# PoolE adds the halves of y_act, one transpose turns all coefficients, ScalarE takes the second norm's variance, and the order of a step is new

## The reference

```python
# 1: linear causal attention over a norm of the channels (eps 1e-6)
q, kv = Wq @ ln_c(x) + bq, Wkv @ ln_c(x) + bkv      # 128 -> 128 and 128 -> 256
Q, K  = elu(q) + 1, elu(k) + 1                       # 8 heads of 16
den = 1.0 / (sum_d(Q * cumsum(K, tokens)) + 1e-10)
num_t = Q_t @ (sum over s <= t of K_s V_s^T)         # causal
x = x + num * den
# 2: mixture of 8 experts, the best 2 of a softmax, over a norm of each token (eps 1e-5)
t = tokens(x); xf = (t - mean(t)) / sqrt(var(t) + eps)
probs = softmax(xf @ gate_w + router_gamma); combine = top 2 of probs, the rest 0
eo = xf @ expert_w[e] + expert_b[e]
t = t + sum_e combine[e] * (gam[e] * eo + bet[e])    # gam, bet are means over instructions
```

## Time and profile before

| what | value |
|---|---|
| times of the runs | 754.3, 754.41, 756.66 us; median 754.41 |
| profiled execution | 755.91 us |
| its span, first to last instruction | 754.1 us |
| PE busy | 717.1 us, 95% |
| DVE busy | 685.9 us, 91% |
| ACT busy | 409.9 us, 54% |
| POOL busy | 397.8 us, 53% |
| DMA | 30.29 MB, 14.4% of 16 engines |
| chain that ended last | PE 91%, DVE 4%, POOL 2% |
| mean granted TensorE clock | 0.982 |

### The profile page before, as it was taken

One profiled execution on the slowest core, in us unless ns is written; L12 is line 12 of the kernel. 1 busy time (PEld: TensorE's weight loads), 2 busy tenths in 40 slices (PEclk: granted clock), 3 DMA queues, 4 the chain that ended last, 5 costly groups with the idle time before them and its releaser, 6 DMA issues.

```text
span 754.1 us, 23195 instructions
## 1 busy us (share of the span) xinstructions
PE 717.1 (95%) x8137; PEld 624.0 (83%) x8137; DVE 685.9 (91%) x2550; ACT 409.9 (54%) x1261; POOL 397.8 (53%) x639
## 2 busy tenths in 40 slices
PE   4767999999999999999999999999999999999986
PEld 2666888888888888888888888888888888888875
DVE  4567999999999999999999999999999999999984
ACT  1122666655555666666665555555555555555544
POOL 5145555555555555555555555555555555555520
PEclk9769999999999999999999999999999999999999
DMA  5101111111111111111111111111111111111101
GB/s 129 33 15 30 42 40 35 37 40 37 39 37 42 42 42 42 42 42 42 42 42 42 42 42 42 42 42 42 42 42 42 42 42 42 42 30 29 30 16 29
DMA packets 60214, 30.29 MB, mean 40 GB/s; under 512 B 2160, under 2 KB 60176, under 8 KB 60176
## 3 DMA queue, kind: packets, MB, share of 16 engines
q1 hardware_dynamic: 60176, 29.79, 14.4%
HBM read 20.34 MB, written 9.44 MB: 39 GB/s over the span
## 4 chain that ended last, share of the span: by engine, by line
PE 91%; DVE 4%; POOL 2%; ACT 1%; issue 1%; DMA 1%; SPq 0%; DVEq 0%; ACTq 0%; POOLq 0%
PE bank L877 11%; PE bank L915 10%; PE bank L894 9%; PE bank L916 9%; PE bank L917 9%; PE bank L933 8%; PE bank L901 4%; PE bank L909 4%; PE bank L884 4%; PE bank L853 3%; PE bank L854 3%; PE bank L855 3%; PE bank L860 3%; PE bank L847 2%; PE bank L866 2%; PE bank L935 2%
## 5 line engine op out<-in xcount | busy, mean ns | idle before, releaser
L574 DVE TENSOR_TENSOR probs<-bank,tri 128x512 f32<-128x512 f32 x288 | 184.9, 684 | 10.2 <-PE bank L877 4.7
L397 ACT ACTIVATE y_act<-bank,scale 128x128 f32<-128x128 f32 x576 | 159.4, 383 | 2.5
L915 PE MATMUL bank<-e_high,x_high 128*128 128x512 f32 x288 | 124.0, 431 | 1.1 <-DVE o L803 1.1
L916 PE MATMUL bank<-e_low,x_high 128*128 128x512 f32 x288 | 113.7, 395 | 0.0
L917 PE MATMUL bank<-e_high,x_low 128*128 128x512 f32 x288 | 113.5, 394 | 0.0
L311 POOL TENSOR_TENSOR qn<-feat,rden 128x512 f32<-128x512 f32 x36 | 38.2, 1061 | 116.4 <-DVE rden L672 116.4
L416 ACT ACTIVATE x_high<-x 128x512 fp32r<-128x512 f32 x36 | 22.8, 633 | 137.0 <-DVE x L664 137.0
L592 DVE SCALAR_TENSOR_TENSOR y_dve<-bank,scale,y_dve 128x128 f32<-128x128 f32 x288 | 92.4, 343 | 0.0
L580 DVE SCALAR_TENSOR_TENSOR qkv<-bank,rstd,b_qkv 128x384 f32<-128x384 f32 x144 | 86.8, 605 | 5.1 <-POOL rstd L301 2.6
L387 ACT ACTIVATE k_odd<-bank,parity 128x512 f32<-128x512 f32 x36 | 24.7, 687 | 114.4 <-PE bank L860 114.4
L933 PE MATMUL bank<-ident,y_act 128*128 128x128 f32 x576 | 80.8, 273 | 1.6 <-ACT y_act L397 1.6
(11 more groups left out here) (139 smaller groups left out, 1764.5 us busy)
## 6 DMA issues: line engine op xcount, KB each, us to landing
x<-in_x SPq DMA_DIRECT2D x36, 256.0 KB, 3.3
x_res<-in_x SPq DMA_DIRECT2D x36, 256.0 KB, 3.2
out<-o SPq DMA_DIRECT2D x36, 256.0 KB, 2.4
beta_raw<-in_L_ffn_beta_w SPq DMA_DIRECT2D x1, 512.0 KB
e_raw<-in_L_ffn_expert_w SPq DMA_DIRECT2D x1, 512.0 KB
w_raw<-in_L_conv_Wkv SPq DMA_DIRECT2D x2, 64.0 KB, 2.4
b_qkv<-in_L_conv_bkv SPq DMA_DIRECT2D x1, 128.0 KB, 4.4
w_raw<-in_L_conv_Wq SPq DMA_DIRECT2D x1, 64.0 KB, 2.6
```

Of the source, the lines that this page charges most:

```text
L397: last = nc.scalar.activation(y_act[:, p, u, e], bank[EXPERTS_AT[u][0]][:, 128 * e:128 * e + 128], ACT.Copy, scale=scale[:, p, u, e:e + 1])
L574: return tt(probs[:, half, i].rearrange("p u e t -> p (u e) t"), bank[SCORES_AT[half][i]][:].rearrange("p (n t) -> p n t", t=T), tri[:].un ...
L915: mm(out, x1_high[:, p, u], e_high[:, w], start=True, stop=False)
L916: mm(out, x1_high[:, p, u], e_low[:, w], start=False, stop=False)
```

## The change

- **Halves.** After `weigh_four` PoolE adds `y_act[2:4]` to `y_act[0:2]` (`add_halves`, 128 x 256 values, one for each unit), and `turn_y` transposes two of `y_act` and one of `y_dve`.
- **Coefficients.** `coef3` is packed (4 units x 4 x 8 columns = 128), so `turn_coef` is one transpose, and `coef_t` 128 x 128. `bias` becomes four fp32r matmuls of 128 columns, each with weights `bias_rows[:, u]` that are zero outside its unit's rows. They are prepared at the start.
- **Variance.** `id_gate` holds the centring matrix for the identity, so the transposed x1 is already without its mean. ScalarE squares each unit with `accum_out` into `mv2` (`variance`); VectorE's `parts` and `moments` of the second norm go.
- **Order.** `LAGS` is 9: x is loaded at lag 0, `turn_x` is at lag 2, `project` 3, `features` 4, keys and denominators 5, scores and values 6, x1 and the router 7, experts and output 8. The banks and the order of every engine are new.

```diff
+REST_COLS = 2 + 6 + EXPERTS + 1 + 1 + 2 * 4
+REST_PSUM = REST_COLS + 1
-LAGS = 6
+LAGS = 9
-AT = dict(x=4, kv=3, att=6, x1_a=6, x1_b=4, k=1, q=7, coef=0, out=1)
-PROJ_AT = (4, 0, 3, 2)
-SCORES_AT = ((3, 7, 2, 0), (0, 5, 6, 7))
-EXPERTS_AT = ((4, 2), (6, 5), (1, 1), (2, 3))
+AT = dict(x=1, kv=5, att=0, x1_a=0, x1_b=5, k=7, q=4, coef=7, out=3)
+PROJ_AT = (2, 6, 2, 1)
+SCORES_AT = ((7, 3, 1, 6), (2, 6, 5, 3))
+EXPERTS_AT = ((4, 1), (4, 3), (0, 7), (5, 4))
+SUMS = 2
@@ PoolE
+            def add_halves(p, u):
+                return tt(y_act[:, p, u, 0:2], y_act[:, p, u, 0:2], y_act[:, p, u, 2:4], ALU.add)
+                    need(pool, "y_act_1", n + 1)
+                    add_halves(p, 1).then_inc(S["y_sum_1"], 1)
...
@@ ScalarE
+            def variance(p, units):
+                for u in units:
+                    last = nc.scalar.activation(squares[:, u], x1_units[u], ACT.Square, scale=CH ** -0.5,
+                                                accum_out=mv2[:, p, u, 1:2])
+                return last
+                if g[7]:
+                    n, p = g[7].i, g[7].par
+                    need(act, "x1_turned", n + 1)
+                    variance(p, (IN_N,)).then_inc(S["x1_var_b"], 1)
+                    need(act, "x1_var_b", n + 1)
+                    nc.scalar.activation(lg_raw[:, IN_N], bank[AT["x1_b"]][:, T:WIDE], ACT.Copy)\
+                        .then_inc(S["lg_raw_b"], 1)
+                    variance(p, range(IN_N)).then_inc(S["x1_var_a"], 1)
...
@@ VectorE, weights
-                make(copy(id_gate[:, 0:T], ident[:]))
+                make(copy(id_gate[:, 0:T], centre[:]))
+                dve.wait_ge(S["rest_pe"], 4)
+                turned = bank[WEIGHTS_AT[3]][:, 0:EXPERTS]
+                make(copy(bias_high[:], turned))
+                for u in range(U):
+                    make(copy(bias_cols[:, u, u, 0:2], bias_high[:].bitcast(F32).unsqueeze(1).broadcast_to([128, 2, EXPERTS])))
+                    make(tt(bias_cols[:, u, u, 2], turned, bias_high[:].bitcast(F32), ALU.subtract))
+                dve.wait_ge(S["rest_pe"], 5)
+                make(copy(bias_rows[:].rearrange("p u d -> p (u d)"), bank[WEIGHTS_AT[0]][:]))
...
@@ PE
             def turn_coef(p):
+                return transpose(bank[AT["coef"]][:, 0:T], coef3[:, p].rearrange("p u s e -> p (u s e)").bitcast(F32), ident[:])
+            def bias(p):
                 for u in range(U):
-                    last = transpose(bank[AT["coef"]][0:3 * QUAD, T * u:T * u + T], coef3[:, p, u].bitcast(F32), ident[:])
-            def bias(p):
-                return mm(bank[AT["out"]][:], e_bias3[:], coef_t[:, p], start=True, stop=False, skip_group_check=True)
+                    last = mm(bank[AT["out"]][:, T * u:T * u + T], bias_rows[:, u], coef_t[:, p], start=(u == 0),
+                              stop=False, skip_group_check=True)
             def turn_y(p, u):
-                for e in range(4):
+                for e in range(SUMS):
```

More of the change, by code:

```diff
@@ L177, in program @@
         names = ("consts setup first_loaded rest_loaded first_pe first_dve rest_pe rest_dve x_eps x1_eps "
[4 rows of a table removed]
-                 "rank_b qkv_0 rank_b_max soft_scaled den_eps hot_b x1 hot_ab rden scale coef qkv_3 x_moments "
[5 rows of a table removed]
-                 "k_sum_3 x_rstd k_sum_4 k_sum_5 k_sum_6 k_sum_7 qk qn state coef_low x_low x1_rstd ").split()
[3 rows of a table added]
+                 "kv_new rank_b_max x1 qkv_2 probs_01 hot_b probs_03 soft_scaled hot_ab x_moments scale "
[3 rows of a table added]
+                 "second feat_0 rank_b soft x_parts out k_sum_0 x1_high q_t exps_0 x1_var_b lg_raw_b x1_var_a "
[3 rows of a table added]
+                 "x_low ").split()
         S = {n: sem(n) for n in names}
@@ new lines, in step @@
+                if g[2]:
+                    p = g[2].par
+                    act.wait_ge(x_loaded[p], 16 * (g[2].half + 1))
+                    nc.scalar.activation(x_high[:, p], x[:, p], ACT.Copy).then_inc(S["x_high"], 1)
+                if g[8]:
+                    n, p = g[8].i, g[8].par
+                    need(act, "coef_turned", n + 1)
+                    need(act, "bias", n - 1)
+                    nc.scalar.activation(coef_t[:, p], bank[AT["coef"]][:, 0:T], ACT.Copy).then_inc(S["coef_t"], 1)
@@ new lines, in step @@
+                if g[7]:
+                    n, p = g[7].i, g[7].par
+                    need(dve, "values_1", n + 1)
+                    need(dve, "values_0", n + 1)
+                    dve.wait_ge(x_res_loaded[p], 16 * (g[7].half + 1))
+                    need(dve, "out", n - 1)
+                    tt(flat(x1, p), bank[AT["att"]][:], flat(x_res, p), ALU.add).then_inc(S["x1"], 1)
+                if g[4]:
+                    n, p = g[4].i, g[4].par
+                    need(dve, "proj_2", n + 1)
+                    add_bias(p, 2).then_inc(S["qkv_2"], 1)
@@ L879, in scores @@
                 return last
-            def from_state(p):
-                for u in range(U):
-                    last = mm(bank[AT["att"]][:, T * u:T * u + T], state[:, U * p + u], q_t[:, p, u],
-                              start=(u == 0), stop=False, skip_group_check=True)
-                return last
             def values(p, half):
@@ L895, in values, with from_state @@
                                       probs[:, half, i, v, e], start=False, stop=(e == 1), skip_group_check=True)
+                return last
+            def from_state(p):
+                for u in range(U):
+                    last = mm(bank[AT["att"]][:, T * u:T * u + T], state[:, U * p + u], q_t[:, p, u],
+                              start=(u == 0), stop=False, skip_group_check=True)
                 return last
@@ new lines, in step @@
+                if g[7]:
+                    n, p = g[7].i, g[7].par
+                    need(pe, "kv_new", n + 2)
+                    need(pe, "x1", n + 1)
+                    if k is not None:
+                        need(pe, "y_act_3", n - 1)
+                    turn_x1(p).then_inc(S["x1_turned"], 1)
+                if g[8]:
+                    n, p = g[8].i, g[8].par
+                    need(pe, "q_t", n + 3)
+                    need(pe, "x1_low", n + 1)
+                    if k is not None:
+                        need(pe, "y_one_3", n)
+                        need(pe, "y_dve_32", n)
+                    experts(p, 1, 0).then_inc(S["experts_10"], 1)
@@ L954, in step @@
                 if g[3]:
                     n, p = g[3].i, g[3].par
+                    need(pe, "x_low", n + 1)
+                    need(pe, "probs_10", n - 2)
+                    if k is not None:
+                        need(pe, "qkv_2", n)
+                    project(p, 0).then_inc(S["proj_0"], 1)
+                if g[8]:
+                    n, p = g[8].i, g[8].par
+                    need(pe, "y_act_0", n + 1)
+                    if k is not None:
+                        need(pe, "q_t", n + 3)
+                    experts(p, 3, 1).then_inc(S["experts_31"], 1)
@@ L1003, in step @@
+                    key_values(p).then_inc(S["kv"], 1)
+                if g[3]:
+                    n, p = g[3].i, g[3].par
+                    need(pe, "probs_11", n - 2)
                     if k is not None:
```

850 lines of the change are left out of this document (410 added, 440 removed), and 18 rows, old and new, of the table names.

## The result

The changed kernel takes 774.61 us (median), the kernel before 755.28 in the same session: a ratio of 1.026 (95% interval 1.021 to 1.030), slower where I had forecast 721.5. The profiled execution of the changed kernel has a span of 774.6 us.

A forecast was written before the change was run, and what follows sets the result against it. PE's own instruction stream was taken as the bound, VectorE close behind. First `o` 95.4 + 29 steps x 18.5 + drain 85.7 + end 3.5 = 721.1 us span, so 721.5 us; range 705 to 744.

The forecast's parts named there:

- PE's stream: PE's instructions in one step: 19.21 - 0.87 (y transposes) - 0.33 (coefficients) + 0.3 (bias) + 0.1 (new order) = 18.4 us.
- The holds: VectorE instructions with two SBUF inputs held by PoolE: 0.5 to 1 us a step in all, said to cost nothing.
- the three instructions that I saw brush against additions: rank_a, second and soft on VectorE, expected to meet PoolE's additions, for 0.5 to 1 us in all.
- VectorE's idle time before `o`: VectorE idles about 1 us before the x parts and before `o`; up to there, being held was to cost nothing.
- My slow rival: VectorE held by PoolE becomes the bound: two full hits a step give 19.5 us (754 us), four 787 us; chance 0.08.
- Does it wait?: Check whether the other engines make PE wait: 0.1 us a step allowed, bounds 0 and 0.6; likeliest step 18.5 us.
- the two narrow starts, x1 and lg_raw_b: VectorE's x1 and causals, ScalarE's square b and lg_raw_b, both ending about when scores 1 starts; 0.1 us a step allowed.
- ScalarE: Four squares with an accumulator on ScalarE, 0.2 to 0.5 us each; its busy share goes from 60% to 65 to 70%.
- Fill: Time to the first `o`: 95.4 us against 89.7, bounds 90 and 102, with PE's first project at about 29.
- Drain: The last six, emptier steps: 17.9, 15.8, 15.5, 14.5, 11.5 and 10.5 us, 85.7 in all, estimates within 6 us.
- Square's table: Rival: Square needs another ScalarE table, two loads a step, PE waits 1.5 to 2.6 us, 780 us or more; chance 0.03.
- PoolE's price: Each of PoolE's four additions of 256 elements takes 0.73 us, 2.9 us more in a step.

The follow-up runs named there:

- experiment 1: The changed kernel with VectorE's lg2 moved ahead of features 1: 747.61 us, ratio 0.989 against the kernel before.
- experiment 3: The kernel before, old order, with the edits one by one: halves 776.89 us, variance (the squares) 777.42, coefficients 754.39, all three 789.53.
- experiments 1 and 4: Experiment 1, and as the other the changed kernel with PoolE's addition into state moved behind k_sum 1: 753.48 us, ratio 0.996.
- experiment 6: The changed kernel with PE's project 3 and key_values ahead of project 0: 765.95 us; with VectorE's y_dve_02 also earlier: 745.10 us.
- the extra matmuls: Experiment 1's kernel with matmuls that nobody reads added where PE idled up to step 7: 742.92 us, ratio 0.982.

## Why the prediction was wrong, point by point

- **PE's stream (0.2 us off, and two errors that cancel in part).** A unit's three transposes now start 0.32 us apart from the next unit's (421.06 and 421.38 below), for 0.54 in the earlier trace rows. The four bias matmuls take 400.97 - 400.58 = 0.39 us; I took 0.53 (0.23 and +0.3) from bounds of 0.44 and 0.90, so even the lower bound was high. PE needs 18.67 us a step once the hold is gone (experiment 1), of which it is idle for 0.17 (99.1 of 100 us busy), for my 18.4. With 0.39 for the bias my sum would have been 19.21 - 0.87 - 0.33 + 0.06 = 18.07. By this estimate the new order costs some 0.4 us, where I had 0.1 and an upper bound of 0.3; which edges cost it isn't traced.

```profile
400.58 0.56 PE L972 MATMUL bank<-coef_t,bias_rows 128*128 128x128 f32 x4
400.97 0.30 PE L893 MATMUL bank<-ident,x 128*128 128x128 f32 x1
```
```profile
421.06 0.38 PE L981 MATMUL bank<-ident,y_act 128*128 128x128 f32 x2
421.27 0.27 PE L983 MATMUL bank<-ident,y_dve 128*128 128x128 f32 x1
421.38 0.38 PE L981 MATMUL bank<-ident,y_act 128*128 128x128 f32 x2
```

- **The holds (the step that failed).** I had the row that shows one and the price, 1.0 us each. I counted only the three instructions that I saw brush against additions, and not each of the fifteen against each PoolE instruction of the step; lg2 against `state` isn't among them. I then covered the sum with VectorE's idle time before `o`. That idle time lies behind the place where PE waits: `qkv_0` stands right after lg2, and project 2 needs it. The small holds by additions that I priced are there, 0.16 us each at lgm and rank_a, and cost nothing: experiment 1 has them too. The one that I left out was 1.1 us in one place and made the step 0.9 us longer (experiments 1 and 4). My slow rival (two full hits a step, chance 0.08) asked for two full hits where one was enough, since it took VectorE's work for the only thing that matters and not its order.
- **Does it wait? (an omission.)** I followed the two narrow starts, x1 and lg_raw_b, and they hold: PE waits 0.2 us before scores 1. add_bias 3's wait for `key_values` I didn't follow. It costs nothing by itself (experiment 1) but brings lg2 beside `state` (experiment 6).
- **ScalarE (right in the new order).** A square takes 0.279 us and its accumulator another 0.208, in my range of 0.2 to 0.5 each. In the old place the same squares cost 0.67 us a step (experiment 3), and in the new order PE has no wait for them in 100 to 700 us.
- **Fill (mechanism right, size off by 14 us).** The first project came at 31.85 for 29, which is within what traces with the same preparation differ by (27.5 to 31.9); steps 3 to 5 took 24.6 for 20, step 6 17.2 for 14.7, step 7 17.4 for 14.3, step 8 18.4 for 17.4. I had summed chains at middle durations, while PE ran at half clock in part and waited, 2.64 us in each of steps 6 and 7, until causal 10 was through. In written-out steps the hand-made order is paid for though the work that it makes room for isn't there. Without the hold the first `o` came 2.2 us earlier, with the extra matmuls 3.7 more, and with key_values earlier too 5.3; the remaining 6 to 7 us against my 95.4 stay unexplained.
- **Drain (off by 8.6 us).** The last six steps took 94.3 us for 85.7; no run was made for this.
- **Square's table, PoolE's price.** Both as forecast: one load, 0.734 us for 0.73.

With the hold taken away the kernel is 1% faster than before and not the 4% forecast: 30 steps give 16 us (19.21 - 18.67 each) and the emptier last five 9 (74.9 for 84.2), but the first `o` comes 17.5 us later (107.2 for 89.7).

## What to carry to other kernels

When an edit puts work on PoolE, or moves anything there, list each VectorE instruction that can be held against each PoolE instruction of the step, and for each overlap ask what stands behind it on VectorE and who waits for that; idle time later in the step is no cover. An order by hand that shows no such meeting is a part of the kernel's speed: the three edits in the old order made it 4.5% slower, by holds and by squares that stand ahead of a copy, and two neighbours swapped in the new one were worth 27 us. A deeper pipeline's fill has waits and a clock of its own; durations of the middle are too short for it.

## What was not expected of the hardware

- The hold ends with PoolE's instruction, whatever the size of VectorE's: 0.18 us became 1.27 (beside a 1.49 us instruction) and 0.34 (beside 0.74). It takes tensor_scalar with one SBUF input too, and neither reductions nor reciprocals.
- It goes both ways: `state` took 1.28 us by itself and 1.34 or 1.49 us in turn when `features` was running as it began (1.57 or 1.72 in most steps of experiment 1).
- Reading the accumulator is an instruction of its own on ScalarE, 0.208 us; square and reading come every 0.25 us (417.87, 418.03, 418.12 in experiment 3's kernel).
- A 128-column fp32r matmul comes every 0.10 us, slightly faster than a 128x128 transpose (0.108: five in 0.54 us in the earlier trace rows).
